# The first expert's first weights split behind the last logits and places instead of amid the last two batches

## The reference: what is computed

```python
x = x + jnp.tanh(g_xattn[0]) * _L0_xattn_ref(_layernorm(x, axis=-1), ctx_2048)
x = x + jnp.tanh(g_ffn[0]) * _L0_ffn_ref(_layernorm(x, axis=-1), L0_ffn_Wg, L0_ffn_w1, L0_ffn_w2)
```

```python
probs = jax.nn.softmax(xr @ Wg, axis=-1)
gate_vals, expert_idx = jax.lax.top_k(probs, K)
...
h = jax.nn.relu(jnp.einsum('ecd,edf->ecf', dispatched, w1))
expert_out = jnp.einsum('ecf,efd->ecd', h, w2)
```

## Time and profile before

| | |
|---|---|
| median of 3 runs | 868.1 us (866.57 to 868.14) |
| profiled execution, span from first to last instruction | 871.2 us |
| first matmul of the first expert | 165.07 us |
| PE busy | 805.5 us (92%) |
| DVE busy | 603.0 us (69%) |
| ACT busy | 357.3 us (41%) |
| POOL busy | 226.6 us (26%) |

### The profile page before, as it was taken

One profiled execution on the slowest core, in us unless ns is written; L12 is line 12 of the kernel. 1 busy time (PEld: TensorE's weight loads), 2 busy tenths in 40 slices (PEclk: granted clock), 3 DMA queues, 4 the chain that ended last, 5 costly groups with the idle time before them and its releaser, 6 DMA issues.

```text
span 871.2 us, 12188 instructions
## 1 busy us (share of the span) xinstructions
PE 805.5 (92%) x4297; PEld 385.8 (44%) x4298; DVE 603.0 (69%) x958; ACT 357.3 (41%) x586; POOL 226.6 (26%) x219
## 2 busy tenths in 40 slices
PE   0589896699999999999999999999999999999996
PEld 0435565344444444444444444444444444444442
DVE  5999998267667786778577667756775677565430
ACT  4988995243404351425242414251425143404310
POOL 3233121666332043104400430033103310332010
PEclk9999998599999999999999999999999999999998
DMA  8704144794637364727452746373626372611000
GB/s 300 281 1 167 73 172 170 188 228 73 150 107 269 119 124 156 243 96 175 156 184 97 144 151 222 97 144 133 241 96 133 123 264 96 112 58 61 1 27 23
DMA packets 79290, 123.17 MB, mean 141 GB/s; under 512 B 43391, under 2 KB 43407, under 8 KB 75169
## 3 DMA queue, kind: packets, MB, share of 16 engines
q1 hardware_dynamic: 68032, 93.33, 35.2%
q0 software_dynamic: 10944, 29.51, 11.8%
q10 hardware_dynamic: 288, 0.00, 0.0%
HBM read 96.53 MB, written 18.95 MB: 133 GB/s over the span
## 4 chain that ended last, share of the span: by engine, by line
PE 82%; DVE 9%; issue 3%; ACT 3%; DMA 2%; another core or an unknown queue 0%; POOL 0%; SPq 0%; ACTq 0%; POOLq 0%; DVEq 0%
PE mm L787 38%; PE mm L857 38%; PE mm L827 2%; PE mm L766 2%; DVE region L1255 1%; PE mm L582 1%; DMA w_stage<-in_ctx 1%; DVE region L1206 1%; DVE region L1277 1%; DVE bn L1192 1%; DVE region L1259 1%; ACT unread L973 1%; DVE w_stage L1255 1%; DVE region L1400 0%; ACT region L983 0%
## 5 line engine op out<-in xcount | busy, mean ns | idle before, releaser
L857 PE MATMUL mm<-region,w_split 128*128 128x512 f16 x1536 | 335.5, 381 | 5.8 <-issue 5.3
L787 PE MATMUL mm<-region 128*128 128x512 f16 x1536 | 335.8, 379 | 0.0
L857 PEld LDWEIGHTS mm<-region,w_split 128*128 128x128 f16 x1536 | 150.7, 98 | 189.2 <-issue 8.9
L787 PEld LDWEIGHTS mm<-region 128*128 128x128 f16 x1536 | 148.8, 98 | 181.3 <-issue 4.2
L1130 ACT ACTIVATE region<-mm 128x512 f16<-128x512 f32 x128 | 76.4, 597 | 312.1 <-PE mm L857 302.6
L1562 DVE SCALAR_TENSOR_TENSOR region<-mm,region 128x512 f16<-128x512 f32 x128 | 88.5, 691 | 119.9 <-ACT region L1130 111.3
L506 POOL DMA_INDIRECT out<-region,back_now x40 | 65.1, 1627 | 168.3 <-DVE region L1575 141.2
L1565 DVE SCALAR_TENSOR_TENSOR region<-w_stage,w_scale,region 128x512 f16<-128x512 f32 x128 | 96.2, 751 | 0.0
L1133 ACT ACTIVATE region<-w_stage,w_scale 128x512 f16<-128x512 f32 x128 | 91.2, 712 | 0.0
L1348 DVE TENSOR_REDUCE top<-w_stage 128x1 f32<-128x512 f32 x112 | 76.0, 678 | 0.0
L1361 DVE SCALAR_TENSOR_TENSOR w_split<-w_stage,w_scale,w_split 128x2048 f16<-128x2048 f32 x32 | 74.4, 2361 | 2.3 <-DVE region L1591 1.6
(11 more groups left out here) (189 smaller groups left out, 576.8 us busy)
## 6 DMA issues: line engine op xcount, KB each, us to landing
w_stage<-in_L_ffn_w SPq DMA_DIRECT2D x64, 1024.0 KB, 5.2
region<-in_x SPq DMA_DIRECT2D x4, 1024.0 KB, 13.6
x_split<-region SPq DMA_DIRECT2D x8, 512.0 KB, 2.9
out<-region SPq DMA_DIRECT2D x4, 1024.0 KB, 5.4
w_stage<-in_ctx SPq DMA_DIRECT2D x2, 1024.0 KB, 12.4
region<-in_ctx SPq DMA_DIRECT2D x2, 1024.0 KB, 15.0
region<-x_split,row_next POOLq DMA_INDIRECT x40
region<-out,row_next POOLq DMA_INDIRECT x40
```

The lines of the kernel that those rows point to most:

```text
L787: mm = pe.matmul(mm2[s % 2][:, :], hidden[:, hh, f, s * P:(s + 1) * P], w2_split[:, wh, f, :], start=(f == 0 and hh + wh == 0), stop=(f == ...
L857: mm = pe.matmul(products(f), w1_split[:, wh, k, f * P:(f + 1) * P], xT[:, xh * KD + k, 0:WIDE], start=(k == 0 and wh + xh == 0), stop=(k ...
```

## The change

Four calls of `split_w1(0, k)` on ACT and four of `low_w1(0, k)` on DVE are written at other places. No call is added, removed or altered, and the lists of PE, POOL and SP stay as they are.

```diff
             copy_turned(3, [0])
-            split_w1(0, 0)
             square_rows(9)
...
             copy_norm(1, [2])
-            split_w1(0, 1)
             copy_norm(1, [3])
             halve(1, 1)
             root(2)
             keep_logits(0)
-            split_w1(0, 2)
             copy_turned(3, [2])
             normalise(2, [0])
-            split_w1(0, 3)
             normalise(2, [1, 2])
...
             keep_logits(2)
+            split_w1(0, 0)
+            split_w1(0, 1)
             exponents()
+            split_w1(0, 2)
+            split_w1(0, 3)
             first_columns(0)
...
             context_down(3)
-            low_w1(0, 0)
             round_rows(3, 1)
             low_rows(1, 0)
             residual(3, [0])
-            low_w1(0, 1)
             norm_scale(2)
             low_rows(1, 1)
-            low_w1(0, 2)
-            low_w1(0, 3)
             residual(3, [1])
...
             places()
             list_loads()
+            low_w1(0, 0)
+            low_w1(0, 1)
+            low_w1(0, 2)
+            low_w1(0, 3)
             gates()
             notes_of_rows()
```

## The result

The median of the kernel after is **875.5 us** (4 executions, 874.09 to 875.92), that of before 868.1; the ratio is **1.0079, 95% interval 1.0068 to 1.0091**. The forecast, 870.4 with a range to 872.9, had the sign and a third of the loss (2.3 of 7.4 us), and lies 5 us too low.

A forecast was written before the change was run, and what follows sets the result against it. The eight experts are a solid TensorE block whose start is set by PE, then DVE, then a relay through POOL's gathers. Terms -0.5 + 0 + 2.8 = +2.3 on the 868.1 median gave 870.4 us, range 866.2 to 872.9.

The forecast's parts named there:

- First term, -0.5: Stretch before the relay, 109 to 149.70: four splits leave ACT and DVE, PE is full, so only 0.5 us gained.
- ACT, nothing: Splits added on ACT behind keep_logits(2) and the exponents end near 153, before the first slot's turn, and cost nothing.
- Third term, +2.8 by the gathers: Relay: POOL's gathers wait for DVE's two-input splits, so PE turns slot 3 at 161.45 instead of 158.68, +2.8 us.
- The rival without a stretch: POOL's gathers in the relay aren't stretched beside the splits; only the first term is left, 867.6 us; chance 0.18.
- the caught first gather: Relay: first split reaches the interface before the first gather, every gather slips 2.3 us more, 872.7; worse-stretch chance 0.12.
- the one in which the change frees more: Before 133, DVE is the real pace and 2.8 us come back instead of 0.5, cancelling the relay's loss: 868.1; chance 0.08.
- Second term: 0: DVE's gates and notes_of_rows end later, but the last note starts at 211.5, as late as now, with 3.7 us cover.
- that PE's half clock cancels: Relay: PE's half clock (0.50) comes with its idle time before and after the change, and cancels.
- The late hand-over: Rival: the 3.9 us stall between PE's last transpose and ACT's copy goes away, gaining 1.6 us: 866.5; chance 0.12.
- The list of what would show it wrong: Signs in the changed profile: gathers keep 1.25, slot 3's copy follows PE at once, or PE waits at turn_rows (L775).

## Why the prediction was wrong, point by point

- **First term, -0.5: right.** `place(0)` (L641) starts at 131.9 for 132.4, and `row_next` is written 0.4 to 0.6 earlier in the two executions. PE is busy for 23.90 of 23.95 and DVE's freed 9.4 us turned into waits (2.82, 2.61, 2.46, 1.36, 1.94, by its rows between 109 and 133, four of the five ended by PE).
- **ACT, nothing: right.** The first copy of a turned slot is at 155.20 (155.44 before), and the pair of splits behind the exponents ends at 152.2.
- **Third term, +2.8 by the gathers: right in kind and size.** Gathers 1.99 and 1.96, 2.30 and 2.26 apart. PE turns slot 3 at 160.80 for 158.43, +2.37, where -0.5 + 2.77 says +2.27; in the second execution it is +2.12. The kernel with the load held has only these terms and measures +1.9 (1.1 to 2.8), where the sum says +2.3. The rival without a stretch is out, as is the caught first gather (1.28 in all kernels). So is the one in which the change frees more: `row_next` came 0.4 to 0.6 earlier and not 2.8.
- **"Second term: 0" is the step that failed.** The forecast had the last note at 211.5 and it came at 211.22; but "as late as now" compared it with 211.90, the figure of the untypical execution. The ordinary one has 205.79, so the notes are 5.4 late and not early. Its cover is 223.18 - 219.83 = 3.35, close to the 3.7 taken, and PE's need moves by 1.91 (225.09 for 223.18). Notes alone: 5.43 - 1.91 - 3.35 = 0.2 of wait. The other 2.0 is what was not thought of at all: the last notes now go behind the start of the load of w2, and the lists land that much later. 5.43 + 2.03 - 1.91 - 3.35 = 2.2, and 2.07 and 2.25 were measured. With the load held there is no wait.
- **The clock behind the new wait,** +1.7 (7.03 for 5.34) in the profile of one execution of the change, was not in the sum either; that PE's half clock cancels was said of the relay only. A further 1.4 us, from the profiled 874.09 to the median, stays without a place.
- **The late hand-over.** It wasn't in the kernel before to begin with (160.59 + 0.33 = 160.93 in its chain), so as a rival it had nothing to gain. The prediction saw that the span lay 3.1 above the median and took it as an offset of the whole. It was these 3.9 us: PE started 4 us late, and the notes, which wait for PE's `mm1_done`, ended 6 us late, so that the notes of the change didn't look late beside them.
- The list of what would show it wrong had the right row at the end: PE waits at `turn_rows` (L775).

## What to carry to other kernels

Work that is moved out of the way of a full engine lands ahead of something: follow what is queued behind it not only to its reader but through every queue that the reader's data passes (here notes, lists, the load of `entries`, `peak_all`, `low_rest`), and take the slack from an execution whose span agrees with the median. A chain of small writes that ends beside a big load is only as early as the load lets it be, and holding that load until they had landed cost nothing measurable here (1.0003). Don't put vector rows with two large inputs beside GpSimd's DMA issue on the way to the first matmul; beside rows with one input the gathers kept their 0.95 us.

## What the runs showed of the hardware

- An indirect DMA on GpSimd that starts beside a two-input DVE row of 128 x 2048 takes 1.95 to 1.99 us instead of 0.95, in every kernel that had such rows beside the gathers, and 2.38 where it starts 0.8 into the first of them. The figures fit a wait for the end of the running row and 0.95 behind it. Beside four one-input rows of the same size it takes 0.95.
- Small list writes landed so that POOL waited 1.65 to 1.66 with the load of w2 held in two kernels, 2.39 and 2.97 in two more, and 3.81 to 7.54 where the load was not held, but for the first profile of before (1.81).
- PE ran its 24 matmuls in 7.03 instead of 5.34 behind waits of 2.25 (granted clock 0.50 from 228.50 to 231.90) and 1.94 (0.50 from 224.90 to 228.30); behind waits of 2.32, 2.07 and 1.82 in other executions they took 5.34. So the length of the wait alone doesn't say which it is.
